# Dummy matmuls of an adaLN transformer layer: 72 instead of 28 per token tile in the first attention loop, none instead of 16 in the second

## The reference, cut to what matters

```python
mod = (_silu(L0_c) @ L0_wmod).reshape(L0_c.shape[0], 6, 1, -1)
sa, ca, ga, sb, cb, gb = (mod[:, 0], mod[:, 1], mod[:, 2], mod[:, 3], mod[:, 4], mod[:, 5])
...
h = _layernorm(x, axis=-1) * (1 + ca) + sa
x = x + ga * attn(h)          # q, k, v; rotary; features sin, cos of a projection
...
kv = jnp.einsum('bhsf,bhsd->bsfd', kp, v)
out = jnp.einsum('bhsf,bsfd->bhsd', qp, kv)
...
h = _layernorm(x, axis=-1) * (1 + cb) + sb
x = x + gb * ffn(h)           # top 2 of 8 experts, and the shared expert
```

## Time and profile before

| what | value |
|---|---|
| median of two runs | 3914.01 us (3908.46 to 3919.56) |
| the profiled execution, its own time | 3913.98 us |
| its span on the slowest core (core 3) | 3912.4 us |
| spans of the eight cores | 3856.7 to 3912.4 us |
| TensorE matmuls, busy in the span | 2617.5 us (67%), 11176 instructions |
| VectorE, busy in the span | 1356.6 us (35%) |

### The profile page before, as it was taken

How to read it: one execution, slowest core, us unless ns; L and a number is a source line. 1 busy time by engine, 2 the same in 40 slices (tenths; PEclk the granted TensorE clock), 3 DMA queues, 4 the chain that set the end, 5 groups by cost and what they waited for, 6 DMA issues and landing times.

```text
span 3912.4 us, 32995 instructions; the slowest of 8 cores (3856.7 to 3912.4 us)
## 1 busy us (share of the span) xinstructions
PE 2617.5 (67%) x11176; PEld 1123.5 (29%) x11176; DVE 1356.6 (35%) x2504; ACT 379.8 (10%) x422; POOL 171.1 (4%) x294
## 2 busy tenths in 40 slices
PE   3349732424983344493389678986899679976886
PEld 1124311111431111141134233432344234432332
DVE  0456255655622544535522113220222022211203
ACT  0111212121111111102100000000000000000000
POOL 0000000000000100000000000000000000000000
PEclk8559855555995566695589889997899789998997
DMA  9514410100335434710054575349543864457547
GB/s 165 111 43 65 68 27 14 27 17 11 57 51 93 73 77 90 175 23 0 1 111 84 115 242 143 64 83 248 175 92 62 183 213 108 92 108 224 164 72 270
DMA packets 84943, 395.15 MB, mean 101 GB/s; under 512 B 7184, under 2 KB 7440, under 8 KB 75312
## 3 DMA queue, kind: packets, MB, share of 16 engines
q0 software_dynamic: 41536, 208.26, 30.7%
q1 hardware_dynamic: 33696, 146.98, 11.0%
q10 hardware_dynamic: 9552, 37.80, 2.7%
HBM read 538.26 MB, written 46.20 MB: 149 GB/s over the span
## 4 chain that ended last, share of the span: by engine, by line
PE 50%; DMA 25%; DVE 13%; issue 8%; ACT 3%; DVEq 0%; POOL 0%; ACTq 0%; POOLq 0%; SPq 0%
PE pb L1055 23%; PE pb L618 9%; DMA AW<-wmod 8%; PE pb L1131 8%; DMA AW<-w2scr 4%; DMA w2scr<-AW 4%; DMA AW<-w2i 4%; PE pb L923 3%; DMA AW<-w1i 3%; DVE AMS L786 2%; PE pb L429 2%; PE pb L578 2%; DVE AHT L583 1%; PE pb L548 1%; DVE AMS L789 1%
## 5 line engine op out<-in xcount | busy, mean ns | idle before, releaser
L1055 PE MATMUL pb<-AHT,AW 128*128 128x512 bf16 x4608 | 1007.3, 381 | 60.3 <-DMA AW<-w1i 43.7
L1131 PE MATMUL pb<-AW,AOT 128*128 128x512 bf16 x2304 | 592.8, 424 | 282.0 <-DMA AW<-w2i 152.0
L1055 PEld LDWEIGHTS pb<-AHT,AW 128*128 128x128 bf16 x4608 | 450.7, 98 | 616.7 <-issue 84.7
L1131 PEld LDWEIGHTS pb<-AW,AOT 128*128 128x128 bf16 x2304 | 241.6, 107 | 633.2 <-issue 424.4
L618 PE MATMUL pb<-AW,AHT 128*128 128x512 bf16 x1536 | 353.2, 384 | 0.0
L1143 DVE TENSOR_TENSOR AMS<-pb,AMS 128x2048 f32<-128x2048 f32 x40 | 91.7, 2292 | 719.2 <-PE pb L1131 715.4
L578 PE MATMUL pb<-identf,AX 128*128 128x128 f32 x256 | 98.6, 445 | 292.9 <-ACT AX L539 240.9
L429 PE MATMUL pb<-AW,scol 128*1 128x512 bf16 x384 | 138.4, 539 | 135.5 <-DMA AW<-wmod 127.5
L1079 ACT ACTIVATE AMS<-AMS 128x1024 f32<-128x1024 f32 x64 | 67.7, 1057 | 1462.1 <-DVE AMS L1076 1462.1
L1081 DVE TENSOR_TENSOR AMS<-pb,AMS 128x1024 f32<-128x1024 f32 x64 | 78.4, 1225 | 366.9 <-PE pb L1055 366.9
L618 PEld LDWEIGHTS pb<-AW,AHT 128*128 128x128 bf16 x1536 | 143.6, 98 | 184.0 <-issue 27.9
(11 more groups left out here) (150 smaller groups left out, 1742.5 us busy)
## 6 DMA issues: line engine op xcount, KB each, us to landing
AW<-w2scr SPq DMA_DIRECT2D x54, 2048.0 KB, 9.2
AW<-wmod POOLq DMA_DIRECT2D x24, 2048.0 KB, 19.2
w2scr<-AW ACTq DMA_DIRECT2D x18, 2048.0 KB
AW<-w1i POOLq DMA_DIRECT2D x32, 1024.0 KB, 8.4
AW<-w3i POOLq DMA_DIRECT2D x32, 1024.0 KB, 9.3
AW<-w2i POOLq DMA_DIRECT2D x16, 2048.0 KB, 23.4
AX<-xin SPq DMA_DIRECT2D x16, 1024.0 KB, 5.7
AW<-wqt POOLq DMA_DIRECT2D x4, 2048.0 KB, 17.3
```

The lines of the kernel that those rows point to most:

```text
L1055: ins = tt.matmul(pu[:, th * 512:(th + 1) * 512], slot(sl)[:, ic * 128:(ic + 1) * 128], ahtb[:, ic * 1024 + th * 512: ic * 1024 + (th + 1) ...
L1131: ins = tt.matmul(pw[:, ob * 512:(ob + 1) * 512], hebuf[:, hc * 1024 + tau * 128: hc * 1024 + tau * 128 + 128], slot(ws)[:, ob * 512:(ob + ...
```

## The change

`emit_warm` itself is not touched. The call in the first attention loop asks for 72 matmuls instead of 28; the call in the second attention loop is taken out.

```diff
@@ -854,7 +854,7 @@
             emit_ln1_tile(1, t, True, None, lnxsA,
                           lambda: W(ar_x1, "lnxs", 57344, 65536),
                           cacol, sacol, ["col1", "col0"], vr=True)
-            emit_warm(28)
+            emit_warm(72)
         emit_mid_B(0, 7)
@@ -884,7 +884,6 @@
             emit_mid_F(1, t)
             emit_mod_jb(8 + 2 * t)
             emit_mod_jb(9 + 2 * t)
-            emit_warm(16)
         emit_wo_wdma(1)
```

## The result

The changed kernel takes 3940.1 us (median), the kernel before 3920.0 us in the same comparison. The ratio is 1.0052, with an interval of 1.0033 to 1.0070. So it is slower, by some 20 us, and clearly so; 61.6 us and at least 3955 us were forecast. Two thirds of the forecast loss are missing. In some executions of either kernel the cores of one or both dies run at a lower granted clock and the time is up to 8% longer; the ratio and the times of the experiments leave these out, the two medians here do not.

What follows compares the result with a forecast made beforehand. The prediction took one chain through the engines to bound the first loop. 76.4 us of added matmuls less 14.8 us of cover gave 61.6; 3914.0 + 61.6 + 0 = 3975.6 us, range 3955 to 3996.

Steps and rivals of the forecast that it cites:

- What bounds the first loop: First attention loop, about 507 us: no engine full, one chain through the engines; a later first L795 lengthens the loop equally.
- The price of the first edit, 76.4 us: First loop: 44 more matmuls in each of eight tiles at the high-clock step of 0.217 us, 9.5 us a tile.
- The cover, 14.8 us: First loop: TensorE's idle time before L795, waiting for L789, absorbs 14.8 us over eight tiles; 61.6 us is left.
- The 5 us that I kept for small matmuls: First loop, L795 and L806: possible gain of 5 us if they run high behind longer blocks; only in the range.
- The second edit at 0: Second loop: the removed blocks (36.2 us) lie wholly in TensorE's idle time before L795, so removal changes 0 us.
- 3914.0 + 61.6 + 0: Whole kernel: time before plus the first edit's uncovered price plus the second edit's nothing, giving 3975.6 us.
- The clock was not carried over: Rival, first loop: the longer block holds TensorE at 2.4 GHz between tiles, gaining 65.3 us, total 3910 us; chance 0.02.
- The added matmuls did not run low: Rival, first loop: added matmuls run at the low clock, price towards 133 us, total 4047 us; chance 0.07.
- Part is given back later: Rival, expert stage: waits for shared DMAs vary between runs, some 15 us either way; chance 0.06 for below 3955.
- The prediction's own sign of being wrong: Wrong if the long blocks' step isn't 0.217 us, L578 or L706 waits shrink, or the second loop moves over 5 us.
- 2%: Whole kernel: a measurement was said to tell about 2% (78 us) from no change; chance 0.92 of landing within.
- the rule that I set aside: Dense matmuls on three cores of a die bring 1.95 GHz: 11.7 us a tile, 3993 us; rejected for the high step.

Runs made afterwards that it cites:

- a_second: The kernel before with only the second edit (28 dummy matmuls in the first loop, none in the second): 3866.8 us, no ratio given.
- a_before: The kernel before, source unchanged (28 and 16 dummies), built again: 3870.9 us, ratio 0.9903 to the kernel before.
- e_after: Both edits (72, none), each instruction's waits ordered own semaphore, DMAs', other engines': 3933.8 us, ratio 1.0025 to the kernel before.
- f_late: The kernel before (28, 16) with TensorE's waits ordered other engines' semaphores first, own next, DMAs' last: 3927.7 us, no ratio given.
- e_order: The kernel before (28, 16) with waits ordered own semaphore, then DMAs', then other engines': 3861.8 us, ratio 0.9815 to the kernel before.

## Why the prediction was wrong, and where it was right

- **What bounds the first loop.** Right. The longer block pushed L795, and VectorE's wait for it appeared (6.83 us in the tile shown).
- **The price of the first edit, 76.4 us.** Right to 3 us: the blocks grew from 65.5 to 139.3 us, by 73.8.
- **The cover, 14.8 us, and no other.** Right. With 36 dummies the loop did not grow; with 72 and one order of waits it grew by 59.3, 60.1, 61.5 and 62.5 us in four pairs. The 5 us that I kept for small matmuls at the higher clock are not needed for any of these, and of L795 and L806 some did run high.
- **The second edit at 0.** Right as far as the noise lets one see: L795's wait for L789 in the second loop became 86.6 us (88 forecast), and a_second's whole time is 4 us below a_before's. In the second loop the cores differ by more than that.
- **The step that failed is the sum, "3914.0 + 61.6 + 0".** It took for granted that what the change leaves alone keeps its time, in 3914.0 as in the loop itself: a term put at nothing. It is not nothing, because the order of waits in a program is not fixed by its source. Against a build in the order that the kernel before seems to have had, the changed kernel had its untouched hand-overs 0.1 us shorter: on core 3 -8.1 us ahead of the first loop, 61.6 - 44.9 = 16.7 us in it, 14.1 in the second loop (part of it may be chance between cores), 6.5 behind. That is 45.4 us, and 61.6 - 45.4 = 16.2 us is what core 3 shows. By the medians over the cores the changed kernel's first loop, 548.4 us, is 4 us above that of the best order (e_after, 544.2), while the 503.3 us of the kernel before are 3 us under that of the worst (f_late, 505.9). By these times the comparison was one of a build with nearly the best order against one with nearly the worst.
- **The rivals.** None happened. The clock was not carried over: L706 took 1.86 or 1.87 us in every tile of the first loop after, as before. The added matmuls did not run low there (44 of them took 73.8 / 8 = 9.2 us, where 9.5 was forecast). "Part is given back later", with the 0.06 for a time below 3955, was right only in its sign; its cause was another.
- **The range** was too narrow by what I did not think of: 3940 lies 15 us below it. The prediction's own sign of being wrong did show: the second loop moved by more than 5 us. Its "2%" for what a measurement can tell was far too wide; the interval of the ratio is 0.2% to either side.

How much of the 20 us is order of waits is inferred. The trace does not show in which order a profiled build has its waits; that the kernel before had a bad one is read from its intervals between transposes, and from f_late, which reproduces three of its stage times to within 3 us. What is shown directly is that order alone moves these intervals, and that in each fixed order the edits cost 56 to 74 us in whole time, about 60 of it in the first loop.

A version faster than both is e_order: the kernel before with each instruction's waits in the best order, 0.9815 of its time (0.9701 to 0.9928). That rests on two runs. A rebuild of the same source alone gave 0.9903 (a_before), and whole times don't show that e_order is faster than this one; its first loop is, by 5 us.

## What to carry to other kernels

Before you explain a difference of one per cent, look at a stage that the change cannot reach: if it moved too, the two programs differ in something that the diff does not show. Order an instruction's waits on purpose, with those that are fulfilled early first and the one that ends last at the end, never by an object's address. Dummy matmuls in front of real ones on an in-order engine are free only up to the idle time that they stand in; beyond it each costs its full step (here 73.8 / 352 = 0.21 us).

## What the runs showed of the hardware

A fulfilled wait is not free when it stands behind the one that ends last. At L578 it costs 0.11 us a pair (1.22 against 1.11 us), at L806 about 0.1 us each (0.80 against 0.61 us with two). The first loop has 64 such pairs and 64 such L806, and with the worst order tried (f_late) it takes 505.9 us against 484.9 us with the best (e_order), 21 us more.

In the changed kernel's profiled execution cores 4 and 5 ran the projections of shift 0 at a granted clock of 0.81, while the other six ran them at 1.00. The same stretch on core 5 and on core 3:

```profile
350.00:450.00 100.00, 100.00 (x365) 36.91 (x364) 40.01 (x97) 12.84 (x22) 2.10 (x4) 0.81 0.32 55
```

```profile
350.00:450.00 100.00, 100.00 (x440) 40.53 (x438) 31.19 (x75) 15.22 (x26) 3.15 (x6) 1.00 0.38 64
```

Sixteen L618 took 4.37 us on core 5 and 3.63 us on core 3, and the first loop of cores 4 and 5 began 37 to 39 us later. In the profiled execution of e_order cores 0 and 1 did the same in both projection stages (0.83 from 300 to 450 us, 0.81 from 1000 to 1100 us), where the other six had 1.00. 0.81 of 2.4 GHz is 1.94 GHz. The Trainium skill ("TensorE: Matmul & The Clock Gate", section "Seeing it yourself") gives 1.95 GHz for a whole die once three of its cores run dense matmuls. So the level of the rule that I set aside does show in this kernel, but in these two traces on two cores of a die and not on all four, and not in every execution: in the kernel before all eight cores came out of this stage within 2 us of each other. What sets it off no run here shows.
